# A third turn of tables for the experts' scattered sums, with six row buffers: a mixture-of-experts layer on one Trainium2 core

## What is computed

```python
h = silu(einsum('ech,ehf->ecf', buf, w_gate)) * einsum('ech,ehf->ecf', buf, w_up)   # F = 96
out = einsum('ecf,efh->ech', h, w_down)
gathered = out[se, minimum(pos, CAP - 1)] * valid[:, None]
y = segment_sum(gathered * w, tok, num_segments=Tn)       # six rows a token, weighted
...
x = layernorm(x + y + shared, axis=-1)
```

## Time and profile before

| | us |
|---|---|
| median of 3 runs | 1128.63 (1125.75 to 1132.01) |
| the profiled execution's own time | 1129.7 |
| its span in the profile | 1127.9 |
| PE busy | 1016.4 (90%) |
| DVE busy | 558.2 (49%) |
| ACT busy | 508.5 (45%) |
| POOL busy | 383.5 (34%) |
| scattered additions, first start to last start | 1009.3 to 1088.9 |
| final loads, first issue | 1092.8 |

### The profile page before, as it was taken

The page is one execution under the profiler, slowest core; times in us unless marked ns, Lnnn a source line. Parts: engine busy times, 40 slices in busy tenths (PEclk is TensorE's granted clock), DMA queues, the critical chain, the costliest instruction groups (busy, mean ns, idle before and its releaser), DMA issues.

```text
span 1127.9 us, 16719 instructions
## 1 busy us (share of the span) xinstructions
PE 1016.4 (90%) x5312; PEld 731.3 (65%) x5312; DVE 558.2 (49%) x1517; ACT 508.5 (45%) x1123; POOL 383.5 (34%) x418
## 2 busy tenths in 40 slices
PE   5789999999999999988899999999999999757826
PEld 4667776777777767666677767777777676434502
DVE  5557655454544544445585564644535435233306
ACT  4435445455454554532344454554545545133312
POOL 4213234535233342022332345352432410135642
PEclk9899999999999999998999999999999999869868
DMA  9611210101001001001111111010000094967558
GB/s 297 186 41 56 62 61 25 45 25 39 15 25 34 24 13 38 16 22 42 41 35 43 45 29 35 29 32 17 25 25 25 11 236 107 252 185 166 88 102 313
DMA packets 78612, 81.90 MB, mean 73 GB/s; under 512 B 13649, under 2 KB 64709, under 8 KB 78528
## 3 DMA queue, kind: packets, MB, share of 16 engines
q1 hardware_dynamic: 65120, 68.77, 20.9%
q0 software_dynamic: 9216, 6.76, 4.0%
q10 hardware_dynamic: 4192, 5.31, 1.5%
HBM read 57.61 MB, written 36.57 MB: 83 GB/s over the span
## 4 chain that ended last, share of the span: by engine, by line
PE 70%; DMA 8%; DVE 8%; issue 5%; SPq 4%; POOL 3%; ACT 2%; ACTq 0%; POOLq 0%; DVEq 0%
PE o_ps L926 20%; PE s_ps L905 15%; PE ring L880 10%; PE ring L915 10%; PE ring L934 8%; DMA sums<-erow,goal_u 6%; PE ring L886 3%; SPq L611 1%; SPq L554 1%; POOL slot_rows L684 1%; PE s_ps L908 1%; DVE neg_max L1095 1%; DVE q_sin L1079 1%; DMA inverses<-inv_t 1%; PE ring L949 1%
## 5 line engine op out<-in xcount | busy, mean ns | idle before, releaser
L926 PE MATMUL o_ps<-pt,v_sb 128*128 128x512 f32 x576 | 294.9, 595 | 5.5 <-DVE ot L1110 5.1
L776 ACT ACTIVATE pt<-ring 128x512 f32<-128x512 f32 x288 | 171.1, 595 | 264.0 <-PE ring L915 253.5
L768 ACT ACTIVATE probs<-s_ps,neg_max 128x128 f32<-128x128 f32 (+7 forms) x256 | 189.6, 741 | 151.6 <-DVE neg_max L1095 141.3
L1095 DVE TENSOR_REDUCE neg_max<-s_ps 128x1 f32<-128x128 f32 (+7 forms) x256 | 191.6, 752 | 114.4 <-PE s_ps L908 114.1
L905 PE MATMUL s_ps<-kt,qt_hi 128*128 128x512 f32 (+3 forms) x768 | 235.4, 388 | 0.0
L915 PE MATMUL ring<-ident,probs 128*128 128x128 f32 x1152 | 175.2, 275 | 5.9 <-ACT probs L768 5.7
L905 PEld LDWEIGHTS s_ps<-kt,qt_hi 128*128 128x128 f32 x768 | 136.5, 191 | 46.1 <-issue 28.8
L915 PEld LDWEIGHTS ring<-ident,probs 128*128 128x128 f32 x1152 | 128.8, 142 | 53.3 <-issue 52.7
L672 POOL TENSOR_TENSOR q_rot<-q_cos,q_sin 128x256 f32<-128x256 f32 x80 | 60.4, 755 | 223.0 <-DVE q_sin L1079 219.8
L905 PE MATMUL s_ps<-kt,qt_lo 128*128 128x512 f32 (+3 forms) x384 | 133.2, 347 | 0.0
L669 POOL TENSOR_TENSOR q_sin<-q_cos,sin_sb 128x512 f32<-128x512 f32 x40 | 51.2, 1280 | 241.2 <-ACT q_cos L742 240.7
(11 more groups left out here) (155 smaller groups left out, 1219.6 us busy)
## 6 DMA issues: line engine op xcount, KB each, us to landing
inv_row<-inverses SPq DMA_DIRECT2D x64, 256.0 KB
fsum<-sums SPq DMA_DIRECT2D x32, 256.0 KB, 6.7
sums<-blank SPq DMA_DIRECT2D x16, 384.0 KB
wexp<-in_L_ffn_w_gate_dram SPq DMA_DIRECT2D x32, 192.0 KB, 6.7
wexp<-in_L_ffn_w_up_dram SPq DMA_DIRECT2D x32, 192.0 KB, 6.9
wexp<-in_L_ffn_w_down_dram SPq DMA_DIRECT2D x32, 192.0 KB, 7.7
slot_rows<-blank SPq DMA_DIRECT2D x1, 5184.0 KB, 28.8
srow<-slot_rows ACTq DMA_DIRECT2D x5, 972.0 KB, 6.0
```

The lines of the kernel that those rows point to most:

```text
L768: act.activation(probs[:, u % 2, h, 0:blocks(u) * P], s_ps[:, n % 2, score_cols(n)], ACT.Exp, bias=neg_max[:, n % 8:n % 8 + 1], accum_out= ...
L776: reader(act.activation(pt[:, n % PTB, :], bank(s), ACT.Copy), s)
L926: pe.matmul(o_ps[:, :], v_sb[:, j, g * D:(g + 1) * D], pt[:, n % PTB, :], start=(j == 0), stop=(j == blocks(u) - 1)).then_inc(pv_done, 1)
L1095: dve.tensor_reduce(neg_max[:, n % 8:n % 8 + 1], s_ps[:, n % 2, score_cols(n)], AX_X, ALU.max, negate=True).then_inc(max_ready, 1)
```

## The change

It adds a third turn, so six tables instead of four, and two more row buffers. Everything that is sized or indexed by `TURNS`, `TABLES` and `EB` follows: POOL's wait looks three scatters back, ACT's six; the blanks are wider (five tables a tile instead of three, six spare parts instead of four); `fsum` has six parts a chunk, so there are 48 final loads instead of 32, six accumulating products for an even chunk and five additions for an odd one. The other edits are needed because 32 is no multiple of 3: `row_base` has 33 columns, SP's waits for the last landings count the scatters of each turn, and ACT indexes the turn by the scatter that it waits for.

```diff
-EB = 4
-TURNS = 2
+EB = 6
+TURNS = 3
 TABLES = 2 * TURNS
...
-        row_base = sb("row_base", [P, PAIRS], F32)
+        row_base = sb("row_base", [P, -(-PAIRS // TURNS) * TURNS], F32)
...
             for n in range(TURNS):
-                sp.wait_ge(erow_sent[n], 16 * (PAIRS // TURNS))
+                sp.wait_ge(erow_sent[n], 16 * len(range(n, PAIRS, TURNS)))
...
-                link(pool.iota(row_base[e * HALF:(e + 1) * HALF, :], pattern=[[0, PAIRS // TURNS], [2 * TABLE, TURNS]],
+                link(pool.iota(row_base[e * HALF:(e + 1) * HALF, :], pattern=[[0, -(-PAIRS // TURNS)], [2 * TABLE, TURNS]],
...
-                used(act, erow_sent[n % TURNS], 16 * ((n - EB) // TURNS + 1))
+                used(act, erow_sent[(n - EB) % TURNS], 16 * ((n - EB) // TURNS + 1))
```

## The result

The changed kernel takes 1123.8 us (median of 14 runs, 1120.8 to 1129.1) against 1127.05 of the kernel before measured beside it: a ratio of 0.9967, with a 95% interval of 0.9951 to 0.9983. That is 3.7 us (1.9 to 5.5) less, a gain, and inside the 0.5% under which this kernel can't be told from no change by a few runs. The forecast was -2.9 us, or 1125.7 us by the three runs of before that it started from.

A forecast was written before the change was run, and what follows sets the result against it. Two turns waiting on scatter landings were taken to pace the experts' stage at 2.32 us a pair. Terms: -22.1 + 5.7 + 1.0 + 10.9 + 1.6 = -2.9 us, median 1125.7 us, range 1118.5 to 1132.

The forecast's parts named there:

- 1 third turn, to POOL's floor: Experts' stage: with scatter n waiting for n-3, no undisturbed wait is left; 31 starts take 57.5 us, not 79.56: -22.1 us.
- term 2: Experts' stage: beside slot and weight transfers, 12 scatters land in 6.2 us, each costing 0.48 us: +5.7 us.
- Term 3: Experts' stage: two late starts of POOL put to issue, untouched by the change: +1.0 us, between 0 and 2.2.
- 4 row buffers: Experts' stage: six row buffers priced at nothing because POOL is the pace; only a reserve against late landings.
- 5 final loads: End: sixteen more loads of 256 KB, 4.19 MB more at 386 GB/s: +10.9 us.
- 6 additions: Final sum: DVE's five additions instead of three show in the tail, +1.6 us; PE's chunk 6 ends beside DVE's additions.
- 7 blanks: Attention and start: wider blanking of the tables fits in and costs nothing; at most 2.5 us if cover is gone.
- A: Experts' stage: every landing grows with the third scatter in flight; 5.2 us slower, 12.5 if strictly serial; chance 0.15.
- B: Experts' stage: some 0.95 us slack a turn swallows the other transfers; -9.6 us (1119.0); chance 0.15.
- C: Experts' stage: PE becomes the pace, rows 2.02 us apart; total between -4 and +1 us; chance 0.10.

The follow-up runs named there:

- t3_quiet: The quiet kernel: changed kernel without loading the last four pairs' weights and the slots of pairs 20 to 31; ratio 0.9914 to the kernel before.
- t3_end4: Changed kernel whose final sum neither loads nor adds the last two tables; ratio 0.9876 to the kernel before.
- the two quiet kernels: Kernel before and changed kernel, each without the last four pairs' weight loads and the slots of pairs 20 to 31; ratios 0.9946 and 0.9914 to before.
- t3_prog2: Changed kernel; in the last four chunks PE and DVE wait per table, and even-chunk statistics precede the next odd chunk's additions; ratio 0.9962 to before.
- t3_both: Changed kernel with late slot and weight transfers spread in pieces, plus per-table waits and reordered statistics at the end; 1120.9 us, ratio 0.9940 to before.

## Why the prediction was right

Term by term, forecast and measured:

| term | forecast | measured |
|---|---|---|
| 1 third turn, to POOL's floor | -22.1 | -21.6 (79.6 to 58.0, t3_quiet) |
| 2 and 3, late landings, late starts | +5.7, +1.0 | +6.4 |
| 4 row buffers | 0 | 0 |
| 5 final loads | +10.9 | +10.3 |
| 6 additions | +1.6 | +1.45 |
| 7 blanks | 0 | 0 |

Terms 1 to 3 share one sum, and the split of the measured ones is that sum's: -21.6 is before with its transfers against t3_quiet without them. With the transfers absent on both sides the third turn is worth 15.6 us.

The starts were forecast to shrink by 15.4 us and shrank by 15.1; the end to grow by 12.5, and it grew by 11.7. The sum of -2.9 stands against -3.7 (-5.5 to -1.9). Both halves are large and nearly cancel, and each was tested by itself (t3_end4, the two quiet kernels). The mechanism held: the turn's wait paced two turns, POOL's issue paces three where nothing disturbs, and the loads set the end. That the sum is within 1 us of the measured one is in part luck, since the starts of kernels alike in this stage differ by up to 2.8 us.

Four things in it were less right than the sum. The late landings were pictured as twelve scatters at 6.2 us, 0.48 us each. There were seven late starts, one of which, behind a landing of 8.0 us, carried 3.3 of the 7: two bursts met there, the chunk of slots at 1015.88 and the weights at 1018.00. The engines' work was split wrongly: by queue the transfers take 14.5 us of it in the kernel before, not 12.0, and a scatter beside them 1.0 us, not 1.2. Only the whole, 27.4 us, entered the argument, and only to say that the engines are full; the price came from twelve times 0.48. So term 2 owes its size in part to luck, with the wrong pattern under it. Term 3 took 1.0 us for late starts of POOL's own; in the quiet kernel no start is more than 0.3 us late, so the term wasn't there, and the transfers' 6.4 us stand against 5.7 and 1.0 together. And term 6 held chunk 6's sum on PE to be out of the way, and asked what a low clock does of chunk 6 alone. In the changed kernel chunk 6's sum did stay out of the way, but chunk 4's took 7.12 us, and once DVE starts earlier PE is the next thing: t3_prog2 waited 2.03 us for chunk 4's sum, t3_both 3.2 us for chunk 6's.

Of the rivals, A (landings grow with the third scatter) fell as a pace: median landing 3.9 us with three in flight, none above 4.3 from 1046.96 on, and 58.0 us in the quiet kernel. Beside the transfers the longest landings did grow, from 6.2 to 8.0 us, and what made them grow is open. The Trainium skill's rule that it drew on ("DMA: Bandwidth & Descriptors", Latency and other measured facts: the fixed cost is mostly the receipt and grows under load) goes the way that landings went beside the transfers, though 8.0 us is 4.2 above the undisturbed 3.8, and the prediction's estimate from the rule was 1.8; no run shows how much of a landing is receipt. A third scatter alone, 3.9 us at an engine share of 0.63, did not lengthen it. B (slack swallows the transfers) fell by the quiet kernels: 6.4 us lost with three turns, 6.0 with two; with a fourth turn most of it is swallowed, 60.2. C (PE the pace) fell too: in the quiet kernel PE kept up with POOL at 1.85. The 341 GB/s that the Trainium skill ("DMA: Bandwidth & Descriptors", Bandwidth) gives for a 1 MB DMA was again not what pieces of 256 KB did, queued one behind the other: 388 GB/s.

## What to carry to other kernels

Here a chain of dependent DMAs that take turns was paced by (landing + restart) / turns, until the issue itself was the pace. In such a chain, find that floor before adding turns, and price what each turn adds elsewhere, here 12 us of the end a turn. Depth of buffers is not depth of turns: the view named the buffer, and only the turn mattered. Where two large terms cancel, measure each with the other left out, since the total can't show either.

## What was not expected of the hardware

The first scatter's start, after 1 ms of the same attention, varied by 5.1 us over fourteen profiles (1004.2 to 1009.3), more than the change moved the total. And the same transfers cost two and three turns the same 6 us, although only three have slack; a fourth turn, with 1.85 us more of it, lost only 2.2 us against the quiet kernel. The longest landings beside the transfers were 7.6 to 8.4 us in the kernels with three turns and 6.2 to 7.4 in those with two, and no run shows why.
